# Product keys: fewer candidates, half of the first head's sums on ScalarE, later gates

## The reference, cut to what matters

```
q = (xn @ w_q.T).reshape(b, t, H, 2, DK)                 # H = 8 heads, two halves
sim1 = einsum('bthd,hkd->bthk', q[..., 0, :], keys[:, :, 0, :])   # 32 keys
sim2 = einsum('bthd,hkd->bthk', q[..., 1, :], keys[:, :, 1, :])
s1, i1 = top_k(sim1, 8);  s2, i2 = top_k(sim2, 8)
all_sc = s1[..., :, None] + s2[..., None, :]             # 64 candidates
fs, pk = top_k(all_sc, 8)                                # the 8 experts of 1024
hidden = gelu(einsum('btd,bthkd->bthk', xn, expert_down[fi]))
hidden = hidden * relu(fs)
out = einsum('bthk,bthkd->btd', hidden, expert_up[fi])
```

## Time and profile before

| | |
|---|---|
| median of 3 runs | 2973.08 us (2970.48 to 2977.26) |
| profiled execution | 2972.85 us, of which the span from first to last instruction is 2971.1 us |
| VectorE busy | 2417.7 us, 81% of the span |
| TensorE busy | 2209.6 us, 74% |
| GpSimd busy | 1745.9 us, 59% |
| ScalarE busy | 1586.5 us, 53% |
| `weigh`, each of the two layers | 279.2 + 40.8 us on VectorE |
| GpSimd `form`, each of the two layers | 422.8 us |

### The profile page before, as it was taken

The page is one execution under the profiler, slowest core; times in us unless marked ns, Lnnn a source line. Parts: engine busy times, 40 slices in busy tenths (PEclk is TensorE's granted clock), DMA queues, the critical chain, the costliest instruction groups (busy, mean ns, idle before and its releaser), DMA issues. The chain is left out here.

```text
span 2971.1 us, 58220 instructions
## 1 busy us (share of the span) xinstructions
PE 2209.6 (74%) x16012; PEld 1656.4 (56%) x16013; DVE 2417.7 (81%) x5792; ACT 1586.5 (53%) x3023; POOL 1745.9 (59%) x1493
## 2 busy tenths in 40 slices
PE   5437777778589999693378876888888377888886
PEld 2112222247478888583256655777777245777775
DVE  6599999956478888554678866999999668999998
ACT  3556666626445555263245544666666225666665
POOL 1589999906400000172445544999999008999996
PEclk9769999978889999697689996999999658999999
DMA  2000000031300000112000001000000000000001
GB/s 53 0 0 1 0 0 0 0 93 41 88 1 1 0 0 1 39 51 54 0 2 1 0 1 33 1 0 0 0 0 0 4 0 1 0 0 0 0 0 29
DMA packets 49009, 36.69 MB, mean 12 GB/s; under 512 B 8137, under 2 KB 44066, under 8 KB 48802
## 3 DMA queue, kind: packets, MB, share of 16 engines
q1 hardware_dynamic: 42658, 23.67, 2.9%
q0 software_dynamic: 5120, 10.50, 1.3%
q10 hardware_dynamic: 1120, 1.22, 0.2%
HBM read 23.83 MB, written 11.53 MB: 12 GB/s over the span
## 5 line engine op out<-in xcount | busy, mean ns | idle before, releaser
L1689 POOL TENSOR_TENSOR k7a_psums<-k7a_sims 128x1024 f32<-128x1024 f32 x224 | 422.8, 1912 | 189.1 <-ACT k7a_sims L1795 158.7
L1689 POOL TENSOR_TENSOR k5a_psums<-k5a_sims 128x1024 f32<-128x1024 f32 x224 | 422.8, 1912 | 75.2 <-ACT k5a_sims L1795 45.8
L1749 PE MATMUL k7a_pw<-g_ident,k7a_w 128*128 128x128 f32 x2048 | 272.6, 279 | 87.8 <-DVE k7a_hid L1881 47.9
L1749 PE MATMUL k5a_pw<-g_ident,k5a_w 128*128 128x128 f32 x2048 | 272.2, 279 | 85.3 <-DVE k5a_hid L1881 48.3
L807 POOL TENSOR_TENSOR mc_hc<-mc_h,mc_cs 128x512 f32<-128x512 f32 x256 | 319.6, 1269 | 13.1 <-PE mc_y L697 5.1
L1749 PEld LDWEIGHTS k7a_pw<-g_ident,k7a_w 128*128 128x128 f32 x2048 | 223.6, 142 | 147.8 <-DVE k7a_w L1872 92.1
L780 DVE TENSOR_TENSOR_SCAN mc_h<-mc_dA,mc_dbu 128x512 f32<-128x512 f32 x256 | 306.0, 1215 | 0.0
L1749 PEld LDWEIGHTS k5a_pw<-g_ident,k5a_w 128*128 128x128 f32 x2048 | 223.4, 142 | 145.3 <-DVE k5a_w L1872 89.5
L1872 DVE SCALAR_TENSOR_TENSOR k5a_w<-k5a_psums,k5a_best,k5a_lift 128x1024 f32<-128x1024 f32 x224 | 279.2, 1270 | 0.5 <-ACT k5a_lift L1810 0.4
L1872 DVE SCALAR_TENSOR_TENSOR k7a_w<-k7a_psums,k7a_best,k7a_lift 128x1024 f32<-128x1024 f32 x224 | 279.2, 1270 | 0.2
L1810 ACT ACTIVATE k7a_lift<-k7a_psums 128x1024 f32<-128x1024 f32 x224 | 227.8, 1027 | 87.2 <-DVE k7a_w L1872 85.8
(11 more groups left out here) (530 smaller groups left out, 6051.8 us busy)
## 6 DMA issues: line engine op xcount, KB each, us to landing
e_w<-in_L_ffn_W_dram SPq DMA_DIRECT2D x16, 256.0 KB, 6.0
token_rows<-e_zn SPq DMA_DIRECT2D x16, 256.0 KB, 3.4
e_zn<-token_out SPq DMA_DIRECT2D x16, 256.0 KB, 5.0
g_X<-in_L_attn_a_x_dram SPq DMA_DIRECT2D x8, 256.0 KB, 6.7
out_dram<-g_X SPq DMA_DIRECT2D x1, 2048.0 KB, 8.7
e_zs<-token_rows,e_token POOLq DMA_INDIRECT x80, 2.5
token_out<-e_ys,e_token POOLq DMA_INDIRECT x80, 2.3
k5p_wq<-in_L_ffn_w_q_dram SPq DMA_DIRECT2D x4, 256.0 KB
```

Source lines behind the costliest of these rows:

```text
L1689: nc.gpsimd.tensor_tensor(psums[:, h - 1, :, :], rows_of(p, h), s2, ALU.add).then_inc(pooled, 1)
L1749: ins = nc.tensor.matmul(pw[:, j, :], w[:, h % WR, j * P:(j + 1) * P], env.ident[:, :], start=(h == 0 and j % 4 == 0), stop=(h == HD - 1 a ...
```

## The change

Three things change, all in `product_keys`.

1. Of the 64 candidates per head, those whose ranks i and j cannot be among the best eight are dropped: the first two rows keep 8 columns, rows 2 to 7 keep 2, which makes 28. Eight zeros, written once, stand behind them. `cross` becomes two instructions (16 and 12 columns a head) instead of one (64), and `rank` searches 36 columns instead of 64.
2. `form` on VectorE makes 16 of the 32 rows of head 0's sums. ScalarE makes the other 16, one activation a row (Identity with a column of `sims` as its bias), in four groups of four: `sums(q)`.
3. On ScalarE the gates stand behind `raise_(4)` and `raise_(7)` instead of `raise_(3)` and `raise_(4)`. On TensorE the second `hide` moves from before `out` to behind `sum_up(4)`.

```
-            cand = sb("cand", [P, HD, 8, 8])
+            CAND, FLOOR = 28, 8
+            cand = sb("cand", [P, HD, CAND + FLOOR])
+            SHARE, GROUPS = K // 2, 4
+            floored, asummed = sem("floored"), sem("asummed")
...                                                  (gpsimd, cross)
-                    nc.gpsimd.tensor_tensor(cand[:, :, :, :], t1, t2, ALU.add).then_inc(crossed, 1)
+                    for at, rows, cols in ((0, (0, 2), 8), (16, (2, 8), 2)):
...
+                        ins = nc.gpsimd.tensor_tensor(dst, t1, t2, ALU.add)
+                    ins.then_inc(crossed, 1)
...
+                nc.gpsimd.memset(cand[:, :, CAND:], 0.0).then_inc(floored, 1)
...                                                  (tensor, body)
                         sum_up(t, 2)
-                        if not final:
-                            hide(t + 1, 1)
                         if not begun:
                             out(t - 1, t + 1 if final else t + 2)
                         sum_up(t, 3)
                         sum_up(t, 4)
+                        if not final:
+                            hide(t + 1, 1)
...                                                  (scalar)
+                def sums(t, p, q):
+
+                    need(act, s_in, t + 1)
+                    need(act, weighed, (t - 1) * HD + 1)
+                    for i in range(SHARE + q * SHARE // GROUPS, SHARE + (q + 1) * SHARE // GROUPS):
+                        ins = nc.scalar.activation(dsum[:, i, :], sims[:, p, 0, 1, :], ACT.Identity,
+                                                   bias=sims[:, p, 0, 0, i:i + 1])
+                    ins.then_inc(asummed, 1)
...                                                  (raise_, for head 0)
+                        need(act, asummed, GROUPS * (t + 1))
...
+                for q in range(GROUPS):
+                    sums(0, 0, q)
...                                                  (vector, rank and form)
-                        ins = nc.vector.max(best[:, p, h, :], cand[:, h, :, :].rearrange("p i j -> p (i j)"))
+                        ins = nc.vector.max(best[:, p, h, :], cand[:, h, :])
...
-                    nc.vector.tensor_tensor(dsum[:, :, :], rows_of(p, 0), s2, ALU.add).then_inc(dsummed, 1)
+                    nc.vector.tensor_tensor(dsum[:, 0:SHARE, :], rows_of(p, 0)[:, 0:SHARE, :], s2, ALU.add).then_inc(dsummed, 1)
```

More of the change, by code:

```diff
@@ L1694, in cross @@
                     need(pool, ranked, t)
-                    t1 = top[:, :, 0, :].rearrange("p h (i o) -> p h i o", o=1).broadcast_to([P, HD, 8, 8])
-                    t2 = top[:, :, 1, :].rearrange("p h (o i) -> p h o i", o=1).broadcast_to([P, HD, 8, 8])
-                    nc.gpsimd.tensor_tensor(cand[:, :, :, :], t1, t2, ALU.add).then_inc(crossed, 1)
+                    for at, rows, cols in ((0, (0, 2), 8), (16, (2, 8), 2)):
+                        n = rows[1] - rows[0]
+                        dst = cand[:, :, at:at + n * cols].rearrange("p h (i j) -> p h i j", j=cols)
+                        t1 = top[:, :, 0, rows[0]:rows[1]].rearrange("p h (i o) -> p h i o", o=1).broadcast_to([P, HD, n, cols])
+                        t2 = top[:, :, 1, 0:cols].rearrange("p h (o i) -> p h o i", o=1).broadcast_to([P, HD, n, cols])
+                        ins = nc.gpsimd.tensor_tensor(dst, t1, t2, ALU.add)
+                    ins.then_inc(crossed, 1)
                 def tile_sums(t, p):
@@ L1819, in body @@
                         raise_(t, 1)
+                        if not final:
+                            sums(t + 1, 1 - p, 0)
                         raise_(t, 2)
+                        if not final:
+                            sums(t + 1, 1 - p, 1)
                         raise_(t, 3)
                         if not final:
-                            gate(t + 1, 1 - p, 0)
+                            sums(t + 1, 1 - p, 2)
                         raise_(t, 4)
                         if not final:
-                            gate(t + 1, 1 - p, 1)
+                            gate(t + 1, 1 - p, 0)
                         raise_(t, 5)
@@ L1829, in body @@
                             bring(t + 2, p)
+                        if not final:
+                            sums(t + 1, 1 - p, 3)
                         raise_(t, 6)
                         raise_(t, 7)
+                        if not final:
+                            gate(t + 1, 1 - p, 1)
                 bring(0, 0)
@@ L1861, in form @@
                     need(dve, weighed, (t - 1) * HD + 1)
-                    s2 = pmix[:, K:2 * K].rearrange("p (o j) -> p o j", o=1).broadcast_to([P, K, K])
-                    nc.vector.tensor_tensor(dsum[:, :, :], rows_of(p, 0), s2, ALU.add).then_inc(dsummed, 1)
+                    s2 = pmix[:, K:2 * K].rearrange("p (o j) -> p o j", o=1).broadcast_to([P, SHARE, K])
+                    nc.vector.tensor_tensor(dsum[:, 0:SHARE, :], rows_of(p, 0)[:, 0:SHARE, :], s2, ALU.add).then_inc(dsummed, 1)
                 def weigh(t, p, h):
@@ L1893, in statistics @@
                     nc.vector.bn_stats(env.stats[:, t, :], env.X[:, t, :]).then_inc(measured, 1)
+                dve.wait_ge(floored, 1)
                 top8(0, 0)
```

## The result

The changed kernel takes 2921.01 us, the median of 4 runs (2920.76 to 2925.67), against 2972.66 us before (4 runs). The ratio is 0.9828, with a 95% interval of 0.9811 to 0.9845. Every ratio here is to the kernel before, timed in the same session. Forecast were 2928 us and a range of 2918 to 2953. The gain of 51.7 us was forecast as 45.4.

A forecast was written before the change was run, and what follows sets the result against it. VectorE was taken as the bound, GpSimd close behind. Saving 0.76 us a tile over 31 tiles in two layers gives 47.1 us, less 0.7 and about 1 at the starts, 45.4: 2928 us, range 2918 to 2953.

The forecast's parts named there:

- VectorE is the bound, 0.76 us a tile: In the product-key layers, form saves 0.525 us and rank 0.235 a tile; VectorE's tile falls from 15.23 to 14.47.
- ScalarE: Sixteen added activations at 0.21 us apiece make ScalarE's tile 12.6 us, under 14.47; it would bound from 0.33 apiece.
- The order: In ScalarE's queue raise 4 has 1.4 us of room, and raise 0 behind the second gate has 0.43.
- GpSimd: The cross as two instructions takes about 0.75 us a tile; GpSimd becomes the bound only from 1.37.
- The start: In each layer weigh 0 comes 3.4 us later; the second cross hides all but 0.7 us in k5.
- the 1 us taken for a late gate: At the layers' start the second gate waits for a hide behind a late weigh 4: about 1 us lost.
- rival E: Better layer start: VectorE's wait and finish's wait for TensorE both go, up to 3 us a layer, 2922; chance 0.12.
- The sum: 31 tiles at 0.76 us in each of two layers, 47.1, less 0.7 and about 1: 45.4 us gained.

The follow-up runs named there:

- the run above: The changed kernel with each of the two cross instructions on GpSimd made three times, the extra two into an unread buffer: 2969.61 us, ratio 0.9987.

## Why the prediction was right, point by point

- **VectorE is the bound, 0.76 us a tile.** Right. The tile went from 15.23 to 14.46, forecast 14.47. The form gave 15.23 - 14.69 = 0.54 for 0.525, the rank 0.23 for 0.235, each alone on the chip.
- **ScalarE.** Right, in both numbers: 0.2125 us apiece for 0.21, and full at 28 or 24 of them as 9.2 + n x 0.2125 says. The Trainium skill's figure ("ScalarE: Activation LUTs", What ACT_TABLE_LOAD costs), an estimate of 0.214, agrees with the trace here: the page's 0.307 for one of these activations stands beside a mean of 307 ns:

```profile
L1816 ACT ACTIVATE k7a_dsum<-k7a_sims 128x32 f32<-128x32 f32 x512 | 120.9, 307 | 0.2
```

  Its rule to add on VectorE would have cost 35 us here, because VectorE was the bound and ScalarE was not.
- **The order.** Right. The room behind the second gate was forecast as 0.43; 0.44 is what the trace shows, and eating it up costs time though ScalarE has time in total. The gates' move is worth nothing alone and 11.0 us with the sums.
- **GpSimd.** Right: the two cross instructions take 0.69 us from start to start (2.06 for the three pairs of the run above) where 0.75 was forecast, and with 7 x 1.87 + 2.06 = 15.15 us of work GpSimd set the tile at 15.15.
- **The start.** Wrong, and nearly all of the difference that is the change's. The step that failed is "0.7 us of the delay is left in k5 and nothing in k7", and the 1 us taken for a late gate. Forecast was a loss of 1.7; tile 3 begins 2.9 us (k5) and 4.2 us (k7) earlier, where three shorter tiles give 2.3, so the start gained 0.6 and 1.9. Weigh 0 is delayed by 3.5 us in k5 and 4.5 in k7 (forecast 3.4): it comes 9.9 us after the first scores in place of 6.3 and 5.4. Rank's wait for the second cross is gone, as forecast. What the sum left out is a second wait, that of finish for TensorE in the next tile. In k7 it was 2.94 us; in k5 it was 1.93, which the prediction didn't look at:

```profile
1845.24 1.28 DVE L1881 TENSOR_TENSOR k5a_hid<-k5a_gl,k5a_pw 128x512 f32<-128x512 f32 x2 [1.93 <-PE k5a_pw L1749]
```

  In the changed kernel it is 0.27 in k5, and there is none in k7. For k7 that adds up: 4.45 - 3.53 - 2.94 - 2.3 = -4.3, against the measured -4.2. So this is rival E, which had named k7 alone. The traces tie the wait to TensorE's clock. In k7, busy time and granted clock (the third number from the end) before, around the wait of rank for the second cross (it ended at 2479.58) and behind it:

```profile
2475.00:2482.00 7.00, 2.16 (x17) 1.69 (x18) 3.47 (x11) 2.30 (x5) 7.00 (x5) 0.92 0.00 0
2482.00:2490.00 8.00, 6.55 (x27) 5.18 (x28) 5.03 (x6) 4.49 (x5) 8.00 (x5) 0.64 0.00 0
```

and in the changed kernel, 0.4 us farther from the first scores:

```profile
2449.00:2456.00 7.00, 6.84 (x49) 6.19 (x48) 6.91 (x19) 6.90 (x17) 7.00 (x6) 0.84 0.00 0
2456.00:2464.00 8.00, 6.39 (x49) 5.19 (x47) 7.87 (x23) 7.93 (x19) 8.00 (x6) 1.00 0.00 0
```

  Before, VectorE stood still for the cross, TensorE was busy 2.16 of 7 us, and its clock in the next 8 us was 0.64, so part of it was spent at 1.2 of the 2.4 GHz; finish then waited 2.94 us for it. Now VectorE comes later and runs through, TensorE stays busy, the clock is 1.00 in the second stretch (it was down earlier, 0.84 over the first), and the wait is gone.

  The other traces separate the two. Each of the fourteen has two starts. In eight of these 28 the clock was at half for part of the time between 18 and 26 us after the first scores (both layers of before, of the candidates alone and of the gates alone; k7 of the two kernels with sums and old gates), and there finish waited 1.53 to 2.94 us. In the other 20 it waited 0.47 at most. A stand of VectorE alone doesn't bring the wait: with the cross made three times rank stood 1.42 and 1.41 us, the clock was at 1.00 throughout that stretch, and finish waited 0.27 us and not at all. The changed kernel with the old gates shows both cases in one execution, k5 first, two stretches each:

```profile
1838.10:1842.10 4.00, 2.11 (x18) 1.63 (x16) 3.25 (x10) 4.00 (x9) 4.00 (x3) 1.00 0.00 0
1842.10:1846.10 4.00, 3.74 (x26) 2.92 (x26) 3.75 (x3) 3.53 (x5) 4.00 (x3) 1.00 0.01 4
2460.50:2464.50 4.00, 2.08 (x17) 1.61 (x16) 3.38 (x11) 3.98 (x10) 4.00 (x3) 1.00 0.00 0
2464.50:2468.50 4.00, 4.00 (x18) 2.86 (x17) 3.62 (x3) 2.55 (x4) 4.00 (x3) 0.58 0.00 0
```

  TensorE was busy about the same in the first stretch of each (2.11 and 2.08 of 4 us), the clock fell in k7 alone, and finish waited 0.27 and 1.53. So the second wait goes with the clock. What brings the clock down isn't shown: VectorE had stood longer in k5 (1.61 us) than in k7 (1.22).
- **The sum.** The layers gave 50.0 for 45.4: 4.2 of the difference are the starts, 0.4 the tiles. Some 2 us of the measured gain lie ahead of the layers and belong to no step. That 2921 comes so near to rival E's 2922 is in part luck: E's full 6 us did not come, and those 2 us filled in.

## What to carry to other kernels

Count an engine's tile from start to start, not by the durations shown, and the tile time after a change of work can be forecast closely (14.47 against 14.46 us here); then ask of every other engine at how many us a tile it takes over. Beside the total, give each added instruction its place in the queue: four more small activations a tile, put into the groups (20 rows), let the tile fall to 14.35 us as counted; put before the last gate, they cost 0.34 us a tile, 0.20 of it by the order and 0.14 through TensorE's clock. A delay at the start of a pipeline is free only while another engine is later still. Once that cover is used up it can cost more than its own length: with 20 rows, 0.84 us more at weigh 0 became 1.6 and 2.3 us at tile 3.

## What had not been expected of the hardware

- With sixteen to twenty-eight activations of 32 columns a tile, each costs 0.212 to 0.215 us from start to start, whether four, five, six or seven stand together; six of them fill 1.28 us.
- At the start of a layer VectorE's wait for TensorE went with TensorE's clock and not with how long VectorE had stood before: 1.53 to 2.94 us in the eight starts with the clock at half shortly before, at most 0.47 in the 20 others.
- Four activations before the last gate brought an uneven rhythm in which TensorE's clock fell in every third tile and the tiles took 14.66, 14.67 and 15.08 us in turn, so one tile read alone would have misled. None of the other thirteen kernels has such a rhythm.
